# Attention and a binary network on one core: steps ordered in pairs, and banks chosen by an estimate of when they are read

## What is computed

```
xn = layernorm(x)                                  # 4 x 2048 x 256
q, k, v = split(xn @ w_qkv + b_qkv)                # 16 heads of 16
scores = where(j >= i, q k^T / 4, -inf)            # per head 2048 x 2048
s = (softmax(scores) @ v) @ w_out + b_out
h = s0 * [xn, -xn] @ (+-1: 512 x 1024);   h = 2 relu(h)
h = s1 * h @ (+-1: 1024 x 1024);          h = 2 relu(h)
g = silu(s2 * h @ (+-1: 1024 x 256))
out = x + s * g
```

## Time and profile before

| | us |
|---|---|
| time, median of 3 runs | 2555.39 (2551.57 to 2561.85) |
| the profiled execution's own time | 2555.14 |
| its span, from the first to the last instruction | 2553.4 |
| PE / DVE / ACT / POOL busy | 2455.9 / 1823.4 / 1542.0 / 913.5 |
| granted TensorE clock, mean | 0.983 |

### The profile page before, as it was taken

How to read it: one execution, slowest core, us unless ns; L and a number is a source line. 1 busy time by engine, 2 the same in 40 slices (tenths; PEclk the granted TensorE clock), 3 DMA queues, 4 the chain that set the end, 5 groups by cost and what they waited for, 6 DMA issues and landing times.

```text
span 2553.4 us, 50994 instructions
## 1 busy us (share of the span) xinstructions
PE 2455.9 (96%) x17616; PEld 1478.7 (58%) x17616; DVE 1823.4 (71%) x4516; ACT 1542.0 (60%) x3135; POOL 913.5 (36%) x1080
## 2 busy tenths in 40 slices
PE   7989999999999999999999999999999999999986
PEld 6877555555555555555555555555555555555552
DVE  7767867677777777777777777777767777777712
ACT  5652656666666666666666665666666665666642
POOL 1014223332433434243433433343434434343532
PEclk9998999999999999999999999999999999999986
DMA  8981111011111212131212212121212122121321
GB/s 317 356 328 45 39 29 53 21 53 29 52 35 40 74 47 69 41 86 34 77 43 69 58 35 79 44 78 41 78 36 81 42 55 67 43 73 42 95 88 47
DMA packets 157805, 192.67 MB, mean 75 GB/s; under 512 B 65276, under 2 KB 102076, under 8 KB 157560
## 3 DMA queue, kind: packets, MB, share of 16 engines
q1 hardware_dynamic: 156600, 189.41, 24.4%
q10 hardware_dynamic: 960, 0.00, 0.0%
HBM read 112.13 MB, written 76.14 MB: 74 GB/s over the span
## 4 chain that ended last, share of the span: by engine, by line
PE 86%; DMA 4%; DVE 3%; ACT 2%; POOL 2%; issue 2%; SPq 1%; POOLq 0%; ACTq 0%; DVEq 0%
PE b_ps L1083 21%; PE b_pv_ps L1061 21%; PE b_ps L1029 18%; PE b_ps L1041 11%; PE b_ps L1080 5%; PE b_ps L1087 5%; PE b_ps L1106 3%; DMA a_xs<-L_attn_x 2%; ACT b_probs L1141 1%; PE a_qk_ps L290 1%; DMA b_xs<-L_attn_x 1%; DVE a_stats L396 1%; DVE a_qk_parts L434 1%; DVE b_part_max L1196 1%; PE b_ps L1049 1%
## 5 line engine op out<-in xcount | busy, mean ns | idle before, releaser
L1141 ACT ACTIVATE b_probs<-b_ps 128x512 f32<-128x512 f32 (+3 forms) x2560 | 1216.9, 534 | 687.2 <-PE b_ps L1029 684.8
L1196 DVE TENSOR_REDUCE b_part_max<-b_ps 128x1 f32<-128x512 f32 x1536 | 976.9, 682 | 296.3 <-PE b_ps L1041 295.0
L1193 DVE CUSTOM_DVE_ANT_0 b_ps<-b_ps,k_mask 128x512 f32<-128x512 f32 (+3 forms) x1024 | 483.2, 515 | 255.0 <-PE b_ps L1041 251.6
L1061 PE MATMUL b_pv_ps<-b_probs,k_vst 128*32 128x512 f32 (+3 forms) x5120 | 604.6, 544 | 12.7 <-issue 8.6
L1029 PE MATMUL b_ps<-k_qst,k_kst 50*128 50x512 f32 (+3 forms) x2560 | 594.2, 461 | 6.2 <-DMA k_qst<-b_max_parts 3.2
L1029 PEld LDWEIGHTS b_ps<-k_qst,k_kst 50*128 50x128 f32 x2560 | 239.9, 184 | 548.7 <-DVE b_part_max L1196 193.0
L1083 PE MATMUL b_ps<-b_u_hi,k_w 128*128 128x256 f32 x2048 | 534.3, 296 | 3.9 <-POOL b_u_lo L965 3.8
L1041 PE MATMUL b_ps<-k_kst,k_qst 48*128 48x512 f32 (+3 forms) x2560 | 493.4, 379 | 28.3 <-ACT b_probs L1141 20.7
L1083 PE MATMUL b_ps<-b_u_lo,k_w 128*128 128x256 f32 x2048 | 519.9, 289 | 0.0
L1083 PEld LDWEIGHTS b_ps<-b_u_hi,k_w 128*128 128x128 f32 x2048 | 392.6, 192 | 62.9 <-issue 47.4
L963 POOL CAST b_u_hi<-b_u 128x512 fp32r<-128x512 f32 x256 | 156.1, 610 | 753.4 <-ACT b_u L1169 753.2
(11 more groups left out here) (101 smaller groups left out, 1849.9 us busy)
## 6 DMA issues: line engine op xcount, KB each, us to landing
qk_parts<-a_qk_parts SPq DMA_DIRECT2D x64, 512.0 KB, 3.8
k_kst<-qk_parts SPq DMA_DIRECT2D x384, 64.0 KB, 2.3
k_qst<-qk_parts SPq DMA_DIRECT2D x384, 64.0 KB, 2.3
a_xs<-L_attn_x SPq DMA_DIRECT2D x16, 512.0 KB, 5.6
xn_T<-a_xT SPq DMA_DIRECT2D x16, 512.0 KB, 5.1
v_plain<-a_v_out SPq DMA_DIRECT2D x16, 512.0 KB, 5.0
k_xf<-xn_T SPq DMA_DIRECT2D x32, 256.0 KB, 3.3
b_v_in<-v_plain SPq DMA_DIRECT2D x64, 128.0 KB, 2.6
```

The costliest lines, as they stand in the source:

```text
L1061: mm = pe.matmul(pv_ps[h * VW:(h + 1) * VW, 0:cols], vst[:, kb // TT, kb % TT, h, :], probs[:, s % P_SLOTS, h, 0:cols], start=start, stop= ...
L1141: act.activation(probs[:, s % P_SLOTS, h, 0:cols], ps[:, banks[place, half][0], 0:cols], ACT.Exp, scale=HD ** -0.5).then_inc(exp_done, 1)
L1193: dve.tensor_tensor_reduce(src, src, mask[:, 0:CHUNK - k0 % CHUNK], 1.0, -3.0e38, ALU.add, ALU.max, dst).then_inc(ring_read, 1)
L1196: dve.tensor_reduce(dst, src, AX_X, ALU.max).then_inc(ring_read, 1)
```

## The change

1. `attention_events`: steps are ordered in periods of two, the even step e and the odd one o. All S events get the time of the even step and the places 1.0 and 3.0 (e), 3.2 and 5.1 (o). The M units of both steps are collected and laid on a list of places: 1.1, 1.2, 3.1, 5.0 where there are four, and 5.05 and 1.05 besides where there are five or six. PV of an even step comes two steps behind at 4.0, that of an odd one a step behind at 6.0. The masks, "keep" and "negmax" are moved to fit.
2. `network_events`: the places are 2.0 and 2.1 of each even step, so two spans in a row per period; before step 0 they are 2.0, 4.0, 4.5 and 6.0.
3. `combine_events`: both halves of "project" lie at 1.8 of the same even step; the last chunk's is one step earlier, and rounded up.
4. `banks_of`: instead of first in, first out, a running estimate of the clocks of PE, ACT and DVE (class `Estimate`) gives the time at which each bank will have been read, and the bank with the earliest such time is taken.

So a period's order is S(e) M M | F F | S(e) M S(o) | PV(e-2) | M S(o) | PV(o-2), where before two steps gave S M | F | S M | PV twice.

```diff
@@ -497,11 +497,18 @@
 U_SLOTS = 2
 SIG_PARTS = 8
 
-PV_LAG, M_LEAD = 2, 21
+M_LEAD = 21
 
 LEAD, CATCH_UP = 14, 40
 
 BANKS = 7
+
+
+
+SCORE_PLACES = ((1.0, 3.0), (3.2, 5.1))
+MAX_PLACES = {4: (1.1, 1.2, 3.1, 5.0), 5: (1.1, 1.2, 3.1, 5.0, 5.05), 6: (1.05, 1.1, 1.2, 3.1, 5.0, 5.05)}
+VALUE_PLACES = ((2, 4.0), (1, 6.0))
+NETWORK_PLACES = (2.0, 2.1)
 
 
 def main_steps():
@@ -534,29 +541,42 @@
     return j - M_LEAD
 
 
+def even(t):
+    return t + t % 2
+
+
 def attention_events():
 
     steps, units = main_steps(), max_units()
     out = []
+    in_period = {}
+    for n in range(GROUPS):
+        for u in range(len(units)):
+            t = max_step(n * STEPS + u // PAIRS)
+            in_period.setdefault(t - t % 2, []).append((n, u))
+    place_of = {}
+    for t, those in in_period.items():
+        for place, (n, u) in zip(MAX_PLACES[max(4, len(those))], those):
+            place_of[n, u] = (t, place)
     for n in range(GROUPS):
         base = n * STEPS
         for s, (c, kb, cols, start, stop) in enumerate(steps):
             t = base + s
+            period = t - t % 2
             for pair in range(PAIRS):
-                out.append((t, 2.0 * pair, "S", n, s, pair))
+                out.append((period, SCORE_PLACES[t % 2][pair], "S", n, s, pair))
             if kb < TT * (c + 1):
-                out.append((t + 1, 0.5, "mask", n, s))
-            out.append((t + PV_LAG, 3.0, "PV", n, s))
+                out.append((even(t), 0.5 if t % 2 else 2.5, "mask", n, s))
+            behind, place = VALUE_PLACES[t % 2]
+            out.append((t + behind, place, "PV", n, s))
             if stop:
-                out += [(t + PV_LAG, 3.1, "out", n, c), (t + PV_LAG + 1, 3.6, "keep", n, c)]
-        shared = {}
+                out += [(t + behind, place + 0.05, "out", n, c), (t + behind + 1, 0.0, "keep", n, c)]
         for u, (pair, ib, kc, k0) in enumerate(units):
-            t = max_step(base + u // 2)
-            shared[t] = shared.get(t, 0) + 1
-            out.append((t, 2.0 * (u % 2) + 0.1 + 0.01 * shared[t], "M", n, u))
+            t, place = place_of[n, u]
+            out.append((t, place, "M", n, u))
             if u + 1 == len(units) or units[u + 1][1] // TT != ib // TT:
                 c = ib // TT
-                out += [(t, 2.5, "neg", n, c), (t + 2, 1.0, "negmax", n, c)]
+                out += [(t, place + 0.05, "neg", n, c), (t + 2, 1.9, "negmax", n, c)]
         for at, c, what in ((-32, 3, "load_q"), (-31, 3, "load_k"), (-26, 2, "load_q"), (-25, 2, "load_k"),
                             (-14, 1, "load_q"), (-4, 1, "load_k"), (0, 0, "load_q"), (1, 0, "load_k"),
                             (-12, 3, "load_v"), (-8, 2, "load_v"), (-5, 1, "load_v"), (-1, 0, "load_v"),
@@ -579,8 +599,8 @@
 
 def network_events():
 
-    places = [(t, p) for t in range(-LEAD, 0) for p in (1.1, 3.05)]
-    places += [(t, 1.1) for t in range(GROUPS * STEPS - 6)]
+    places = [(t, p) for t in range(-LEAD, 0, 2) for p in (2.0, 4.0, 4.5, 6.0)]
+    places += [(t, p) for t in range(0, GROUPS * STEPS - 6, 2) for p in NETWORK_PLACES]
     spans = []
     for k in range(PIECES):
         if k == 0:
@@ -616,7 +636,7 @@
 COMBINE = (("fetch", 0), ("fetch_heads", 0), ("bias", 2), ("invert", 3), ("spread", 5), ("scale", 7), ("project", 10))
 COMBINE_LATE = (("fetch", 0), ("fetch_heads", 0), ("bias", 1), ("invert", 2), ("spread", 3), ("scale", 4),
                 ("project", 6))
-COMBINE_LAST = COMBINE_LATE[:-1] + (("project", 5),)
+COMBINE_LAST = COMBINE_LATE[:-1] + (("project", 4),)
 
 
 def combine_events():
@@ -629,41 +649,95 @@
     for e, (t, i, stages) in enumerate(chunks):
         for n, (what, gap) in enumerate(stages):
             if what in ("bias", "scale", "project"):
-                out += [(t + gap + half, 1.0 + 0.001 * n, what, e, i, half) for half in range(2)]
+                out += [(even(t + gap) if what == "project" else t + gap + half, 1.8 + 0.001 * n, what, e, i, half)
+                        for half in range(2)]
             else:
                 out.append((t + gap, 3.7 + 0.001 * n, what, e, i))
 
-    out += [(base + 34, 3.9, "last_weights"), (base + STEPS + PV_LAG, 1.0, "last_sums")]
-    return out + [(base + STEPS + PV_LAG, 2.0 + half, "last_project", half) for half in range(2)]
+    out += [(base + 34, 3.9, "last_weights"), (base + STEPS + 2, 1.0, "last_sums")]
+    return out + [(base + STEPS + 2, 2.0 + half, "last_project", half) for half in range(2)]
 
 
 def in_order():
     events = attention_events() + network_events() + combine_events()
-    events += [(-LEAD - 1, 3.8, "load_bias"), (-LEAD - 1, 3.9, "stored"), (4, 1.5, "spread_bias"), (8, 1.0, "fold_bias")]
+    events += [(-LEAD - 1, 3.8, "load_bias"), (-LEAD - 1, 3.9, "stored"), (4, 1.5, "spread_bias"), (8, 1.8, "fold_bias")]
     return [(what, *args) for _, _, what, *args in sorted(events, key=lambda e: e[:2])]
 
 
+class Estimate:
+
+    STREAM = 2400.0
+    SEEN, FREED = 0.28, 0.18
+    EXP, MAX = (1430.0, 0.119), (960.0, 0.065)
+
+    def __init__(self):
+        self.clock = {"PE": 0.0, "ACT": 0.0, "DVE": 0.0}
+        self.mode = None
+
+    def enter(self, mode):
+        if mode != self.mode:
+            self.clock["PE"] += 0.12 if mode == "V" else 0.207
+            self.mode = mode
+
+    def reads(self, engine, columns):
+        rate, fixed = self.EXP if engine == "ACT" else self.MAX
+        start = max(self.clock[engine], self.clock["PE"] + self.SEEN)
+        self.clock[engine] = start + fixed + columns / rate
+        return self.clock[engine] + self.FREED
+
+
 def banks_of(order):
 
 
 
+    steps, units = main_steps(), max_units()
     out = {}
     last = {}
-    free = list(range(BANKS))
+    release = [0.0] * BANKS
     counts = {"exp": 0, "ring": 0, "f": 0}
+    estimate = Estimate()
+    clock = estimate.clock
+
+    def take(use, kind):
+        bank = min(range(BANKS), key=lambda n: release[n])
+        clock["PE"] = max(clock["PE"], release[bank])
+        release[bank] = float("inf")
+        counts[kind] += 1
+        out[use] = (bank, *last.get(bank, (None, 0)))
+        last[bank] = (kind, counts[kind])
+        return bank
+
     for at, (what, *arg) in enumerate(order):
-        kind, number = {"S": ("exp", HALVES), "M": ("ring", HALVES), "negmax": ("ring", 1), "fold_bias": ("ring", 1),
-                        "project": ("ring", 1), "last_sums": ("ring", 1), "last_project": ("ring", 1),
-                        "F": ("f", 1)}.get(what, (None, 0))
-        for k in range(number):
-            use = ("F", arg[0]) if what == "F" else (at, k)
-            if use not in out:
-                bank = free.pop(0)
-                counts[kind] += 1
-                out[use] = (bank, *last.get(bank, (None, 0)))
-                last[bank] = (kind, counts[kind])
-            if what != "F" or arg[8]:
-                free.append(out[use][0])
+        if what in ("S", "M"):
+            if what == "S":
+                columns = steps[arg[1]][2]
+            else:
+                columns = CHUNK - units[arg[1]][3] % CHUNK
+            estimate.enter("R")
+            taken = [take((at, k), "exp" if what == "S" else "ring") for k in range(HALVES)]
+            clock["PE"] += columns / estimate.STREAM
+            for bank in taken:
+                release[bank] = estimate.reads("ACT" if what == "S" else "DVE", columns)
+        elif what == "F":
+            use, _, _, _, kind, _, lo, hi, end = arg
+            estimate.enter("F")
+            if lo == 0:
+                take(("F", use), "f")
+            clock["PE"] += 0.1177 * (hi - lo)
+            if end:
+                release[out["F", use][0]] = estimate.reads("ACT", 1400 if kind == "L2" else 640)
+        elif what == "PV":
+            estimate.enter("V")
+            clock["PE"] += 4 * steps[arg[1]][2] / estimate.STREAM
+        elif what == "out":
+            clock["ACT"] += 0.5
+        elif what == "recip":
+            clock["DVE"] += 0.46
+        elif what in ("negmax", "fold_bias", "project", "last_sums", "last_project"):
+            estimate.enter("F")
+            bank = take((at, 0), "ring")
+            clock["PE"] += 0.08 if what == "negmax" else 1.73
+            release[bank] = estimate.reads("DVE", 512)
     return out
```

## The result

The changed kernel takes 2477.99 us (median of 4 runs, 2475.53 to 2481.97) against 2555.42 for the one before: ratio 0.9696, 95% interval 0.9672 to 0.9720, 77 us or 3.0% faster. Forecast were 110 us, 2445, in a range of 2395 to 2508. Its profiled execution has a span of 2474.6 us (before 2553.4). Medians and ratios leave out two executions of the kernel before, made beside x1 to x4, that took 3180 and 3506 us at granted clocks of 0.65 and 0.58.

What follows compares the result with a forecast made beforehand. TensorE was taken as the bound, a sequence of starts with 0.90 us a step not streaming. Gains of 96 us for steps 0 to 610, 2 lead-in and 12 end made 110 from 2555.1: 2445 us, range 2395 to 2508.

Steps and rivals of the forecast that it cites:

- The bare transitions: PE's undisturbed junctions between items and stretches in the new order: 1.24 us a period, 0.62 a step.
- Rival 4: Third items' weights not loaded ahead: each second junction 0.12 instead of 0.02, 61 us, 2506; chance 0.02 shared with Rival 5.
- The exit: PE leaving a stretch after three items: bounds 0.12 and 0.20, 0.12 taken; costing more than after two would show error.
- The steady waits, w: PE's waits for PSUM banks in each two-step period of the new order: 0.25 us, between 0 and 1.05.
- The reciprocals' bunching: DVE's eight reciprocals per network piece fall on two periods in ten, some 0.5 lost in each, 0.10 on average.
- the masked maxima: DVE's masked maximum of 512 columns takes 0.71 + 0.14 instead of 0.68 us: 0.1 us a period charged.
- one walk: Bank releases followed through one period, 512 columns everywhere, six banks free after F: an ordinary period loses 0 to 0.1.
- Rival 5: The order does not merge the network's spans; no way seen for it; chance 0.02 shared with Rival 4.
- The two points without slack: The S behind the first PV and the second M before F, where banks come free just in time.
- 1 (the readers keep up, 2385): ACT and DVE empty banks in time, waits of 0.05 a period: 0.645 a step, 2385 us; chance 0.12.
- 2 (half of the gain lost): Bank waits of 0.45 to 0.6 a period, or exits at 0.20: 2505 to 2551, priced at 2515 us; chance 0.15.
- 3 (slower): Rows of items outrun the PSUM readers, 1.05 more wait a period: 2765 us, 2605 with half; chance 0.05.

Runs made afterwards that it cites:

- x1: Changed kernel with the old first-in, first-out choice of banks: 2513.3 us, ratio 0.9838 to the kernel before.
- x4: Changed kernel with the second half of each projection at 4.5 instead of directly behind the first: 2496.2 us, ratio 0.9766 to the kernel before.
- x11: Changed kernel with each reciprocal of a network piece covering one column instead of 64: 2475.5 us, ratio 0.9692 to the kernel before.
- x12: Changed kernel with plain maxima in place of the masked ones: 2473.2 us, ratio 0.9682 to the kernel before.
- x7: Changed kernel with ACT's exp (from the second group on) and DVE's unmasked maxima on half the columns: 2425.8 us, ratio 0.9499 to the kernel before.
- x3: Changed kernel with the network's second span of a period moved to 4.5, so seven stretches instead of six: 2663.1 us, ratio 1.0425 to the kernel before.
- x5: Changed kernel with ACT's exp on half the columns from the second group on: 2460.5 us, ratio 0.9642 to the kernel before.
- x6: Changed kernel with DVE's unmasked maxima on half the columns and exp scaled by 0.001: 2450.6 us, ratio 0.9607 to the kernel before.
- x8: Changed kernel with the product that turns the maxima at 2.2, behind F, instead of 1.9: 2482.5 us, ratio 0.9728 to the kernel before.

## Why the prediction was right in direction and 33 us off in size

- **The bare transitions: right.** 0.12 to the second item, 0.02 to the third, 0.12 for an exit, 0.14 and 0.20 for PV and F. The 1413 period shows each, and the median distances from 800 to 1800 us are 0.12, 0.02, 0.11 to 0.12 (0.18 from the third item to F), 0.14 and 0.20. The second item of a stretch costs 0.12 without any change of shape, as much as an exit, so stretches alone don't price an order. That M behind PV costs what S costs, 0.14, had no row before and held. Rival 4, third items at 0.12, fell.
- **The exit.** I gave the bounds 0.12 and 0.20 and took 0.12. Both occur: 0.11 to PV behind an item in time, 0.21 behind an item that had itself waited (medians of 485 and 101 exits from 300 to 2290 us; it was so in the kernel before, with 0.11 and 0.21). Towards F an item in time leaves after 0.15, where after two items in the kernel before it took 0.12. So what I had named as a sign of being wrong, exits that cost more after three items, did show there. The weight loads (PEld) in front of the S at 1413.66, in time, and of the S at 1415.29, late, show a difference: one begins 0.23 ahead of its matmul, the other 0.03. That this is the cause was not tested. A late item pays twice. This I had not counted.

```profile
1413.43 0.19 PEld L1103 LDWEIGHTS b_ps<-k_qst,k_kst 50*128 50x128 f32 x2
...
1415.26 0.22 PEld L1103 LDWEIGHTS b_ps<-k_qst,k_kst 50*128 50x128 f32 x2 [0.30 <-ACT b_probs L1215]
```

- **The steady waits, w: the term that was mis-sized.** Forecast 0.25 a period, measured 2 x (3.407 - 2.62) - 1.24 = 0.33. The sum for steps 0 to 610 was 96 us; from the first S (234 before, 236.10 after) to the projection at step 610 it is 2158.6 before and 2086.5 after, 72 us. That is 24 of the 33 us by which the forecast was off.
- **Its parts were wrong one by one.** The reciprocals' bunching, 0.10, is nothing (x11); the masked maxima, 0.1, are 0.01 to 0.03 (x12). The ordinary period, at 0.05, loses 0.13 where it really is ordinary. The step of the prediction that failed is that one walk, "with 512 columns everywhere" and with F of 2.6 us in front, stood for every period. Rival 5 even counts the periods with one span, "about one period in six", and charges nothing for them; they lose 0.74 on average against 0.23, which is 0.08 a period, 25 us in all. After each diagonal the PV's are short and S and M are full, and the product's own bank was put at nothing. That w came out as near as 0.25 to 0.33 is luck: two false terms, about 0.2, hid most of the missing ones.
- **The two points without slack** were half right. From 800 to 1800 us the second M before F is 0.06 a period late. The S behind the first PV is only 0.03 late, with 0.02 more at its exit. The largest place is one that the walk had as free, the third item behind F, with 0.07, and the exits towards F add another 0.07.
- **The choice of banks** stood in the figure as given. It is worth 36 us under the new order (x1), almost half of the result, and the prediction could not say so because it walked with the earliest bank for the new order only.
- **The end:** forecast 12 us, measured 8.5 with a scatter of some 2, by the mechanism named (x4).
- **The lead-in:** forecast 2 us; its length scattered between 232 and 239 us over the profiles of these kernels, so nothing can be said.
- **Rivals.** 1 (the readers keep up, 2385) is what x7 shows with lighter readers, 2426. 2 (half of the gain lost) is near what x1 does, 2513. 3 (slower) did not come, but x3 shows that it was close: the same order with F cut in two is 4% slower than before. The point that decides was not the number of items in a row, as I had put it, but the time that PE spends elsewhere between the rows. The Trainium skill, TensorEngine Tiling, PSUM Bottleneck, says that tiling speeds TensorE and not the evacuation of PSUM; x5 to x7 agree, with 14, 23 and 50 us.
- **DVE's share** was to rise to 78%; it rose to 75.9%, in step with the pace.

## What to carry to other kernels

Where PE changes between shapes of the array, count stretches and price them from the distances of starts; here a visit of the network costs 0.12 in and 0.20 out, and a pair that joins a stretch as its third costs 0.02. Then ask what the readers of PSUM do meanwhile: a long stretch that needs no new banks is the time in which they catch up, so here merging it was worth more than its switches, and splitting it cost more. When walking through a schedule to size a wait, walk with the mix of sizes that really meet, above all a short step in front of a full one and the period in which the long stretch is only half as long, and let every added term name the instruction that would be late.

## What the runs showed that I had not expected

- Cutting the 2.6 us F stretch into two of 1.3 us cost 186 us (x3), three times the price of the extra switch, 0.21 x 305 = 64 us.
- A late item costs about 0.10 again at its exit from the stretch: 0.21 instead of 0.11 at the median.
- Moving the product that turns the maxima (x8) moved its wait from in front of F to the third item behind F, and gained nothing.
- Halving ACT's and DVE's reads gave gains that more than add (14, 23, together 50 us), though PE is busy 96% by the page in the changed kernel and in x5, x6 and x7 alike.
- Taking 38 us in 1000 of DVE's work away (x11) changed the time by nothing that can be measured, and taking 179 away where PE waits for it (x6) gave 23 us.
